# Last stage of a macaron layer on eight cores: the next chunk's output projection issued ahead of this chunk's transposes and second FFN

## What is computed

```
def _layernorm(x, axis=-1, eps=1e-5): ...
def _L0_ffn_ref(x, weight):
    b_weight = jnp.sign(weight)
    return jnp.einsum('bsi,oi->bso', x, b_weight)

x = x + 0.5 * ffn(layernorm(x), W)
x = x + attn(layernorm(x), ...)     # state-space block, ends in:
        yn = (yg - mean) / jnp.sqrt(var + EPS)      # per sequence and head
        yn = yn * gn_w + gn_b
        out = yn * jax.nn.silu(z)
        return out @ Wout.T
x = x + 0.5 * ffn(layernorm(x), W)
```

## Time and profile before

| | us |
|---|---|
| median of two runs | 7749.5 (7744.3 and 7754.8) |
| the profiled execution | 7770.4 |
| its span, slowest core (core 6) | 7768.8 |
| spans of the eight cores | 7732.6 to 7768.8 |
| stage 3 on core 6, from the first Wout product | 6009.3 to 7763.6 |

### The profile page before, as it was taken

How to read it: one execution, slowest core, us unless ns; L and a number is a source line. 1 busy time by engine, 2 the same in 40 slices (tenths; PEclk the granted TensorE clock), 3 DMA queues, 4 the chain that set the end, 5 groups by cost and what they waited for, 6 DMA issues and landing times.

```text
span 7768.8 us, 69023 instructions; the slowest of 8 cores (7732.6 to 7768.8 us)
## 1 busy us (share of the span) xinstructions
PE 4163.0 (54%) x17827; PEld 1932.3 (25%) x17827; DVE 3218.8 (41%) x8603; ACT 1770.9 (23%) x3944; POOL 245.4 (3%) x349
## 2 busy tenths in 40 slices
PE   2255555555555555745556556655653554554454
PEld 1122212222222222213333333333331221222222
DVE  2244444444444444534434443444343444444343
ACT  0022222222222222202211221122121222222222
POOL 0000000000000000000000000000000000000000
PEclk9966777676767666766666666666765676767676
DMA  2201111101111111121111111112112121222121
GB/s 33 34 27 33 33 38 37 34 28 38 36 33 33 33 33 33 41 44 36 49 47 33 49 47 36 36 48 48 33 36 65 63 71 63 71 65 73 57 71 46
DMA packets 341890, 342.42 MB, mean 44 GB/s; under 512 B 145761, under 2 KB 276970, under 8 KB 341506
## 3 DMA queue, kind: packets, MB, share of 16 engines
q1 hardware_dynamic: 296034, 201.64, 9.2%
q0 software_dynamic: 45472, 136.37, 7.1%
HBM read 189.09 MB, written 150.99 MB: 44 GB/s over the span
## 4 chain that ended last, share of the span: by engine, by line
PE 32%; DVE 27%; issue 15%; ACT 14%; DMA 9%; DVEq 2%; SPq 1%; ACTq 0%; POOLq 0%; POOL 0%
PE pt L422 5%; PE pb L454 4%; PE pb L722 3%; PE pb L806 3%; ACT G L409 3%; PE pb L739 3%; ACT dumpA L362 3%; DVE G L875 3%; PE pb L1099 3%; PE pb L502 2%; DMA G<-sp_y 2%; PE pb L553 2%; DVE G L429 2%; PE pt L336 2%; DVE G L1051 2%
## 5 line engine op out<-in xcount | busy, mean ns | idle before, releaser
L422 PE MATMUL pt<-identc,G 128*128 128x128 bf16 x1536 | 391.5, 266 | 1698.2 <-ACT G L409 1497.6
L553 PE MATMUL pb<-G,slotB 128*128 128x512 bf16 x2048 | 566.2, 427 | 320.7 <-ACT xpB L511 180.6
L429 DVE COPY G<-pt 128x128 bf16<-128x128 bf16 x1536 | 345.5, 225 | 778.0 <-PE pt L422 636.1
L422 PEld LDWEIGHTS pt<-identc,G 128*128 128x128 bf16 x1536 | 156.5, 105 | 1959.7 <-issue 1958.8
L502 PE MATMUL pb<-G,slotA 128*128 128x512 bf16 x2048 | 570.6, 429 | 0.0
L362 ACT ACTIVATE dumpA<-G 128x512 bf16<-128x512 bf16 x384 | 241.4, 629 | 1204.2 <-DVE G L464 639.2
L817 ACT ACTIVATE G<-pb,colT 128x128 bf16<-128x128 f32 x512 | 188.2, 368 | 1278.1 <-PE pb L806 1240.8
L1075 PE MATMUL pb<-slotB,G 128*128 128x512 bf16 x2048 | 448.9, 380 | 34.2 <-DVE G L1051 34.2
L1046 ACT ACTIVATE acc_s<-G 128x512 bf16<-128x512 bf16 x256 | 161.1, 629 | 1086.2 <-DVE G L1051 1085.8
L553 PEld LDWEIGHTS pb<-G,slotB 128*128 128x128 bf16 x2048 | 197.8, 105 | 687.3 <-issue 632.9
L454 PE MATMUL pb<-wS,G 128*128 128x512 bf16 x1024 | 314.9, 483 | 89.7 <-DVE G L429 89.7
(11 more groups left out here) (160 smaller groups left out, 6129.2 us busy)
## 6 DMA issues: line engine op xcount, KB each, us to landing
sp_xc<-G SPq DMA_DIRECT2D x64, 512.0 KB, 2.9
sp_z<-G POOLq DMA_DIRECT2D x64, 512.0 KB, 3.7
G<-sp_xc SPq DMA_DIRECT2D x64, 512.0 KB, 5.2
sp_y<-G POOLq DMA_DIRECT2D x64, 512.0 KB, 6.2
G<-sp_y SPq DMA_DIRECT2D x128, 256.0 KB, 4.3
G<-sp_z POOLq DMA_DIRECT2D x128, 256.0 KB, 3.8
out<-G SPq DMA_DIRECT2D x64, 512.0 KB, 3.1
G<-x POOLq DMA_DIRECT2D x32, 512.0 KB, 8.8
```

What stands on the lines that cost most here:

```text
L422: emit=lambda e, tt=tt, kt=kt, bank=bank: e.transpose(bank[:, kt * 128:(kt + 1) * 128], src[:, tt * D + kt * 128:tt * D + (kt + 1) * 128], ...
L429: e.tensor_copy(out=dst[:, kt * chunk + tt * 128:kt * chunk + (tt + 1) * 128], in_=bank[:, kt * 128:(kt + 1) * 128]))
L553: last = e.matmul(bank[:], slotB[:, k * INNER + ot * 128:k * INNER + (ot + 1) * 128], u2_rhs(k, pp), start=(k == 0), stop=(k == KD - 1))
```

## The change

`p2_main` is cut into three functions. `p2_main_a` holds the x1 load, the Wout product and x2; `p2_ln` the layernorm; `p2_main_b` the transposes, f2, x3 and the output. The loop is written anew, so that `p2_main_a` of chunk i+1 stands between the layernorm and the transposes of chunk i, and loads and gy of chunk i+1 behind the layernorm of chunk i. Instructions, tiles, banks and sizes stay as they are.

```
-        def p2_main(b, c):
+        def p2_main_a(b, c):
...
-            layernorm(v_x2, kx2, v_utm2, "utm2", par)
+
+        def p2_ln(b, c):
+            par = c % 2
+            layernorm(v_x2p[par], f"x2_{par}", v_utm2, "utm2", par)
+
+        def p2_main_b(b, c):
...
             transpose_u(v_utm2, "utm2", v_ufm2, kuf2, CH_A)
...
             p2_loads(*chunks[0])
             p2_gy(*chunks[0])
+            p2_main_a(*chunks[0])
             for i, (b, c) in enumerate(chunks):
+                p2_ln(b, c)
                 if i + 1 < len(chunks):
                     p2_loads(*chunks[i + 1])
                     p2_gy(*chunks[i + 1])
-                p2_main(b, c)
+                    p2_main_a(*chunks[i + 1])
+                p2_main_b(b, c)
```

More of the change, by code:

```diff
@@ L1059, in p2_main @@
             v_x2 = v_x2p[par]
-            v_ufm2 = v_ufm2p[par]
             v_gy = v_gyp[par]
-            kx2, kuf2, kgy = f"x2_{par}", f"ufm2_{par}", f"gy_{par}"
+            kx2, kgy = f"x2_{par}", f"gy_{par}"
             x1_view = bass.AP(sp_x1.tensor, (b * L + T0) * D,
@@ L1088, in p2_main @@
                              op=ALU.add))
-            layernorm(v_x2, kx2, v_utm2, "utm2", par)
+        def p2_ln(b, c):
+            par = c % 2
+            layernorm(v_x2p[par], f"x2_{par}", v_utm2, "utm2", par)
+        def p2_main_b(b, c):
+            T0 = c * CH_A
+            par = c % 2
+            v_x2 = v_x2p[par]
+            v_ufm2 = v_ufm2p[par]
+            kx2, kuf2 = f"x2_{par}", f"ufm2_{par}"
             transpose_u(v_utm2, "utm2", v_ufm2, kuf2, CH_A)
```

## The result

The changed kernel takes 7899.4 us, the median of 11 runs (7859.6 to 7946.6); the kernel before takes 7754.2, the median of 10 (7744.3 to 7814.7). The ratio is 1.0174, with a 95% interval of 1.0136 to 1.0213. It is slower, by 1.7%, some 145 us at the medians, and not by the 245 of the forecast. The interval lies wholly above 1, so the kernel is slower, though the median ratio is under the 2% that the forecast took as what a measurement can tell.

What follows compares the result with a forecast made beforehand. Stage 3 was held bound by a chain of engines, none full: 55.54 us a chunk, rising to 61.06. 7749.5 + 185 (chain) + 68 (limited clock) - 6 (core 5 below core 6) gave 7996, rounded to 7995; range 7900 to 8050.

Steps and rivals of the forecast that it cites:

- the 245 of the forecast: Whole kernel: predicted slowdown, from 7749.5 to 7995 us.
- near 61: Stage 3 after the change: chunk period predicted at 61.06 us, against 55.54 before.
- 185: Stage 3 on core 6: predicted growth from 1754.4 to 1939.1 us, without any limited clock.
- 1 and 2, to the first multiply: From x3(i-1): layernorm(i) 6.34 us, then silu and table load on ScalarE 4.82; gy(i+1) starts at 11.16.
- 3, to the product: VectorE makes gy(i+1), then TensorE starts the Wout product: 12.69 us.
- Step 4: Wout product(i+1) on TensorE, now in the chain and starting at clock 0.50: 16.13 us.
- Step 5: Transposes(i) and copies(i), until f2 starts: 8.93 us, carried over from before the change.
- f: Chain part in the kernel before: transposes and copies until f2 starts, 8.93 us.
- Step 6: f2(i), x3(i) and mean wait for the output DMA, f2 starting at clock 0.50: 12.15 us.
- The rival that the clock holds through the transposes: TensorE keeps clock 1.00 into f2, which takes 7.0 us; each chunk 2.4 shorter, 7858 us; chance 0.08.
- The 68 for a limited pair: Stage 3 on die 1: clock 0.81 lengthens products 2.2 us a chunk, 68 over 31 chunks; chance 0.47.
- the case without a limited core: Rival: no core has its clock limited in stage 3; 7935 us, chance 0.28.

Runs made afterwards that it cites:

- halved products: 8 of 16 k-steps of the Wout product left out: in the changed kernel 7679.9 us, in the kernel before 7759.9 us.
- warm-up: Changed kernel plus 18 unread TensorE matmuls on weights, released by gy's fourth multiply, ahead of the product: 7816.5 to 7943.8 us, ratio 1.0128.
- silu: Changed kernel with the first silu of chunk i+1 issued ahead of layernorm of chunk i: 7858.9 to 7950.7 us, ratio 1.0136.
- warm-up and silu: Changed kernel with both the 18 unread matmuls and the first silu of chunk i+1 ahead of layernorm(i): 7868.1 to 7926.9 us, ratio 1.0185.
- gy ahead: Changed kernel with loads and gy of chunk i+2 issued ahead of the layernorm of chunk i: 7403.8 us, ratio 0.9533.

## Why the prediction was right and wrong

**The direction and the mechanism were right.** Product(i+1) stands in the chain, and what the new order saves (the x2, the apply, the wait for y) is less than what it adds. The halved products show the first (195 us against none), the layernorm moved alone the second: that half of the edit gains 2.1 a chunk, and the product's place turns it into a loss. The period was to be near 61 and is 58.4: f2 of the first chunk starts at 6060.69 and that of chunk 30 at 7812.59 on core 3, over 30. From product(0), which starts at 5994.58, to the last x3, which ends at 7852.87, stage 3 takes 1858.3, 104 more than the 1754.4 of before, where the forecast had 185; the period's (61.06 - 58.40) x 31 = 82 are the difference.

The steps of the forecast, the chunk shown, and the mean of 30 chunks of core 3:

| step | forecast | chunk shown | mean |
|---|---|---|---|
| 1 and 2, to the first multiply | 11.16 | 10.93 | 11.06 |
| 3, to the product | 12.69 | 12.69 | 12.38 |
| 4, product, to the transposes | 16.13 | 15.53 | 15.69 |
| 5, transposes and copies, to f2 | 8.93 | 8.24 | 8.27 |
| 6, f2, x3 and output | 12.15 | 10.63 | 10.97 |
| sum | 61.06 | 58.02 | 58.37 |

**Steps 1, 2 and 3 were right.** In the chunk shown the shift is ready 6.09 after x3 (forecast 6.34), the multiply comes 4.84 later (4.82), and the product 12.69 after that (12.69). ScalarE's silu and not y releases the first multiply, by 2.50. Together 23.62 against 23.85. On the mean it is 23.44; the 12.69 of the chunk shown is the upper end of 12.33 to 12.69.

**Step 4, the product, failed in size:** 15.53 against 16.13, which was the mean of four first products. The mechanism (it starts at 0.50, rises, then runs at the full clock) is shown by the windows and by the warm-up, which takes it to 13.97. But its length is no constant. From its start to the first transposes it took 15.24 to 16.70 in the 30 chunks, and in the two experiments that shorten the time ahead of it (x3 buffer, silu) it grew by 0.7. So no fixed length for it, 16.13 or another, holds in more than one order of work.

**Step 5, transposes and copies, failed in size:** 8.24 against 8.93. I carried f over from the earlier trace rows, where the transposes ran at 0.50. Directly behind the product they have 1.00, as the third window shows, and 16 of them take 5.44; in the chunk of the earlier trace rows they took 6.15. The forecast's own remark that no row of before has transposes directly behind a product was the place to take something off. I used this gap only for a rival about f2.

**Step 6, f2, x3 and the output, failed in size, and by most:** 10.63 in the chunk shown against 12.15, and 10.97 on the mean. The clock was right: f2 starts at 0.50 in the window. But the low clock ended sooner in it, 3.7 after f2's start where it was 4.7 in the chunk of the earlier trace rows: f2 took 8.85 instead of 9.38, and from its start to the end of the second x3 it took 6.30 on the mean instead of 6.74 (core 6 before). And the wait for the output DMA was 94.6/30 = 3.15 on the mean instead of 3.88, and 2.87 in this chunk. All eight cores show the shorter wait. The traces point to where it comes from. In the kernel before, most of these waits are 2.9 too, but in two clusters of chunks most are 4 to 6. One of those, on core 6, and the DMA queues in its time (6440.90 to 6446.60; packets, MB, share):

```profile
6445.99 0.69 DVE L1108 SCALAR_TENSOR_TENSOR G<-pb,G 128x512 f32<-128x512 f32 x1 [5.06 <-DMA out<-G]
...
q1 hardware_dynamic: 144, 0.52, 23.2%
q8 instruction: 1, 0.02, 1.7%
```

The 144 packets are the output (512 KB). The one of q8, 16 KB, is of the kind "instruction". Of the 256 output waits of the kernel before (32 chunks, 8 cores), the 115 during which a packet of q8 was under way last 4.7 on the mean, the 141 others 2.9. In the changed kernel 15 waits meet one of q8 (4.1) and 31 one of q14, the other queue of that kind (3.6); the other 210 last 2.9. In 88 of the 115 the packet starts 1.0 to 2.3 after the second x3, when an undisturbed output is still being written too (its last packet ends 2.4 after it), so the longer wait is not what catches the packet. That the packet holds up the output is inferred from this coincidence. The 3.88 was therefore no property of the step, but of where in the chunk these packets fell, and the new order moved them elsewhere. For the forecast that was bad luck. Taking the wait away altogether gained about 10 us.

The rival that the clock holds through the transposes did not happen, and that its 7858 is so near the 7863 of the runs without the limit is chance. The clock fell in the course of transposes and copies (1.00 in the third window, 0.50 in the fourth), and f2 never took 7. The Trainium skill, "TensorE: Matmul & The Clock Gate", Part 4, says that transposes don't count as busy for the clock; the fall agrees with it. It came before TensorE paused, in the last of the transposes, which end at 7809.79:

```profile
7809.50:7809.80 0.30, 0.27 (x1) 0.10 (x1) 0.23 (x1) 0.00 (x0) 0.00 (x0) 0.50 0.00 0
```

**The 68 for a limited pair failed its own test, and its size is open for this kernel.** No core of the profiled execution shows 0.81 anywhere. Seven of 11 runs have a die at a lower mean clock, and their median is 7929.0, 66 above the 7863 of the rest, but none of them was traced, and that the two numbers agree proves little: the limit costs time in stages 1 and 2 as well. The nearest trace, the changed kernel with the second x3 buffer, shows both parts. Its core 3 had 0.81 for 529 us of stage 3 and ended 7961.0 - 7837.0 = 124 behind core 5, which had no limit. 67 of the 124 had arisen before stage 3 began and 57 arose in it (1905.9 against 1849.4). The price for a product was right: 16.96 against 13.97 in the run with warm-up and silu, the 3.0 of the earlier trace rows. What varies is for how many chunks it is paid. (The forecast also names cores 6 and 5 as the last of the kernel before; core 7, at 7762.8, stood between them. Nothing rests on it.) So the time is a mixture: the case without a limited core (7935 in the forecast) came out at 7863, the runs with one (7995) at 7929, and the median of 7899.4 depends on how many of the 11 runs were of which kind.

So what failed is the size of steps 4 to 6, above all of step 6. They were all carried over from rows taken in another context, and all were too long, by 0.60, 0.69 and 1.52 in the chunk shown and by 0.44, 0.66 and 1.18 on the mean. With the period as it is, the forecast's own sum for no limited core comes to 7935 - 82 = 7853, and 7863 was measured.

## What to carry to other kernels

When engines run in the order of the code, ask of every step that is moved forward whether its input is made in the same turn; if it is, move the input a turn further first (7404 us instead of 7899 here, by the same order of TensorE). When durations of TensorE are carried over to a new order, look at what the engine does just before them: the same product took 14.0 or 15.7 us, and transposes with their copies 8.9 or 8.2. When a mean wait is carried over, look whether it is made of two kinds of chunks, and what the long ones have in common. And where a gain ahead of TensorE's work does not reach the time, look for it in the length of that work at the lower clock.

## What was not expected of the hardware

- The silu ahead, 1.4 us a chunk less of idle time ahead of the product, was worth 6 us over the stage with the product starting at 0.50 (1849.7 against 1856.0) and 43 us with it starting at 1.00 (1765.9 against 1808.7).
- Three kernels that differ in what they save ahead of the product have the same chunk period, 58.0 us, as long as it starts at 0.50.
- An output DMA that lands after 2.9 us otherwise took 4.7 on the mean when a single 16 KB packet of the instruction queue q8 was under way with it.
- 18 matmuls without a use, in time in which TensorE idled, made the kernel faster by 43 us.
- The limit takes a die's cores in pairs. Five traces show 0.81 (the kernel before, half the product, gy ahead, second x3 buffer, warm-up with silu). It comes and goes on cores 0 and 1, 2 and 3, 4 and 5, or 6 and 7 together; in three of them never on both pairs of a die at once, in the other two (half the product, second x3 buffer) on both for 140 to 290 us. The clearest is the warm-up with silu. With the mean clock at 0.708 on all four cores of the die, cores 0 and 1 ended at 7896 and 7870, and cores 2 and 3 at 7770 and 7782. In stage 3 a product had 0.81 on core 0 and 1.00 on core 2. In stage 1, from 500 to 3200 us, it was the other way round: mean clock 0.77 on cores 0 and 1 and 0.70 on cores 2 and 3.
